# Query row loads of an attention visit: from SyncE's queue into ScalarE's instruction order

## The reference

```
for i in range(NL):                       # NL = 6, D = 128, H = 16 heads of HD = 8
    xn = _adaln(x, noise_emb, n1_w[i], n1_b[i])
    q, k, v = jnp.split(xn @ qkv_w[i].T, 3, axis=-1)
    q = _rope(q.reshape(B, L, H, HD)); k = _rope(k.reshape(B, L, H, HD))
    a = _attn(q, k, v.reshape(B, L, H, HD), src_mask).reshape(B, L, D) @ so_w[i].T   # softmax(q k / sqrt(HD)) v
    x = x + a
    ...   # the same against the 77 context rows (cross attention), then a GELU feed-forward
```

## Time and profile before

| what | value |
|---|---|
| three runs, median (lowest, highest) | 2218.05 us (2217.97, 2221.16) |
| profiled execution, its own time | 2213.04 us |
| its span, first to last instruction | 2211.2 us |
| PE busy | 1802.6 us (82%) |
| DVE busy | 1723.1 us (78%) |
| ACT busy | 1517.0 us (69%) |
| POOL busy | 1035.1 us (47%) |
| DMA traffic | 155.11 MB, mean 70 GB/s |

### The profile page before, as it was taken

How to read it: one execution, slowest core, us unless ns; L and a number is a source line. 1 busy time by engine, 2 the same in 40 slices (tenths; PEclk the granted TensorE clock), 3 DMA queues, 4 the chain that set the end, 5 groups by cost and what they waited for, 6 DMA issues and landing times.

```text
span 2211.2 us, 40093 instructions
## 1 busy us (share of the span) xinstructions
PE 1802.6 (82%) x13138; PEld 767.3 (35%) x13138; DVE 1723.1 (78%) x4125; ACT 1517.0 (69%) x2808; POOL 1035.1 (47%) x1506
## 2 busy tenths in 40 slices
PE   4564185278999999999999999999999999999662
PEld 2332174122333333333333333333333333333231
DVE  6766111588899888998888987889988889888777
ACT  2443031156888888888888887888888888889553
POOL 2443712824454555454554554554545545444532
PEclk9766598569999999999999999999999999999785
DMA  3001122322423343423533325333244232432100
GB/s 101 1 0 38 56 86 76 85 52 69 96 66 67 88 101 79 92 59 70 108 82 83 79 55 112 86 68 88 53 106 94 71 81 68 90 86 59 30 2 20
DMA packets 153736, 155.11 MB, mean 70 GB/s; under 512 B 32247, under 2 KB 137523, under 8 KB 153523
## 3 DMA queue, kind: packets, MB, share of 16 engines
q1 hardware_dynamic: 151487, 148.34, 28.8%
q0 software_dynamic: 2048, 4.20, 0.7%
HBM read 82.15 MB, written 67.85 MB: 68 GB/s over the span
## 4 chain that ended last, share of the span: by engine, by line
PE 55%; DVE 10%; DMA 9%; POOL 6%; ACT 5%; issue 3%; SPq 2%; POOLq 0%; DVEq 0%; ACTq 0%
PE ps L1357 14%; DMA q<-scratch_queries 8%; PE ps L1310 7%; PE ps L1321 6%; DVE smax L1878 4%; PE ps L1459 4%; PE ps L1469 4%; ACT big L1586 4%; PE ps L1368 3%; PE ps L1433 2%; PE ps L600 2%; PE ps L610 2%; PE ps L1393 2%; PE ps L1344 2%; PE ps L1332 1%
## 5 line engine op out<-in xcount | busy, mean ns | idle before, releaser
L1586 ACT ACTIVATE big<-ps 128x512 f32<-128x512 f32 x1920 | 1009.6, 613 | 214.9 <-PE ps L1321 204.6
L1878 DVE TENSOR_REDUCE smax<-ps 128x1 f32<-128x512 f32 x1536 | 966.7, 684 | 175.8 <-PE ps L1310 123.3
L1357 PE MATMUL ps<-big,vaug 128*32 128x512 f32 x3072 | 430.4, 634 | 2.3 <-ACT xnT L1594 1.2
L1310 PE MATMUL ps<-k,q 49*128 49x512 bf16 x1536 | 294.7, 394 | 80.9 <-DMA q<-scratch_queries 56.1
L1321 PE MATMUL ps<-q,k 52*128 52x512 bf16 x1536 | 291.1, 392 | 9.2 <-DVE smax L1878 3.3
L1310 PEld LDWEIGHTS ps<-k,q 49*128 49x128 bf16 x1536 | 76.1, 94 | 314.4 <-DVE smax L1878 153.1
L1789 POOL CAST mparts<-smax 128x16 bf16<-128x16 f32 x96 | 19.2, 200 | 324.4 <-DVE smax L1878 324.4
L1886 DVE TENSOR_REDUCE maxima<-ps 128x4 f32<-128x308 f32 x384 | 157.2, 469 | 9.4 <-PE ps L1344 5.9
L1321 PEld LDWEIGHTS ps<-q,k 52*128 52x128 bf16 x1536 | 78.9, 94 | 215.5 <-issue 65.4
L1775 POOL TENSOR_TENSOR rot<-rot,cs 128x512 f32<-128x512 f32 x72 | 92.0, 1277 | 103.3 <-DVE rot L1897 103.3
L1780 POOL TENSOR_TENSOR hat<-rot,rparts 128x512 f32<-128x512 f32 x72 | 82.6, 1161 | 70.6 <-ACT rparts L1634 70.6
(11 more groups left out here) (312 smaller groups left out, 2938.2 us busy)
## 6 DMA issues: line engine op xcount, KB each, us to landing
k<-scratch_keys SPq DMA_DIRECT2D x48, 384.0 KB
q<-scratch_queries SPq DMA_DIRECT2D x48, 384.0 KB, 8.1
cq<-scratch_cross_queries SPq DMA_DIRECT2D x48, 384.0 KB, 6.0
scratch_keys<-rparts SPq DMA_DIRECT2D x24, 384.0 KB, 2.5
scratch_queries<-rparts SPq DMA_DIRECT2D x24, 384.0 KB
scratch_cross_queries<-rparts SPq DMA_DIRECT2D x24, 384.0 KB
scratch_keys<-rparts SPq DMA_DIRECT2D x24, 256.0 KB, 2.2
scratch_queries<-rparts SPq DMA_DIRECT2D x24, 256.0 KB
```

Of the source, the lines that this page charges most:

```text
L1310: last = nc.tensor.matmul(out[u], m.q6[rows, v % 2, 2 * g + pr, qt * P:(qt + 1) * P], m.k6[rows, v % 2, 2 * g + pr, :], start=True, stop=True)
L1357: last = nc.tensor.matmul(m.ps[32 * j:32 * j + 32, pv_bank, :], of_head(m.vaug, v % 2 * TB + kt, g, j), of_quad("self", q)[:, j, :], start ...
L1586: nc.scalar.activation(of_quad(kind, p // 2)[:, p % 2 * 2 + u, :], bank("exp" if kind == "self" else "cross exp", p, u), ACT.Exp, scale=sc ...
L1878: nc.vector.tensor_reduce(m.smax[:, n % 2, qt, u, pr:pr + 1], bank("max", i, u), AX.X, ALU.max).then_inc(s_read["self"], 1)
```

## The change

The two query loads leave SP's program and become a piece of ACT's, "ACT load queries", with the same number in the plan as before (-32643 in the part "next"). In ACT's order this puts them behind exp 13 of visit v - 1 and ahead of scale cross of visit v - 2 (visits 4 to 23). Their waits go with them. The two DMAs of the mask rows stay on SP and move into load_keys, ahead of the two key loads. So SP's order becomes mask, mask, key, key where it was key, key, mask, mask, query, query. No arithmetic changes and no bytes.

```diff
-    "SP load queries": (-32643,),
+    "ACT load queries": (-32643,),
...
-            def load_queries(v):
+            def load_keys(v):
                 b, i = v % B, v % 2
+                sp.wait_ge(x_stored["key"], 48 * (v + 1))
                 if v >= 2:
                     sp.wait_ge(scores["self"], PER_VISIT * (v - 1))
                 for u in range(2):
                     lo = u * ROW_BLOCK
                     sp.dma_start(m.k6[lo + ROW_MASK:lo + ROW_SHIFT, i],
                                  a["neg_mask"][b:b + 1, :].unsqueeze(1).to_broadcast([1, PAIRS, S])).then_inc(k_loaded[i], 16)
-                sp.wait_ge(x_stored["query"], 48 * (v + 1))
-                src = a["queries"][b].rearrange("(i u r) c n -> u (r c) i n", u=2, r=HD)
-                for u in range(2):
-                    sp.dma_start(m.q6[u * ROW_BLOCK:u * ROW_BLOCK + ROW_MASK, i], src[u]).then_inc(q_loaded[i], 16)
-
-            def load_keys(v):
-                b, i = v % B, v % 2
-                sp.wait_ge(x_stored["key"], 48 * (v + 1))
-                if v >= 2:
-                    sp.wait_ge(scores["self"], PER_VISIT * (v - 1))
                 src = a["keys"][b].rearrange("(i u r) c n -> u (r c) i n", u=2, r=HD)
                 for u in range(2):
                     sp.dma_start(m.k6[u * ROW_BLOCK:u * ROW_BLOCK + ROW_MASK, i], src[u]).then_inc(k_loaded[i], 16)
...
-                for i in due("SP load queries", now):
-                    load_queries(i)
...
+            def load_queries(v):
+                b, i = v % B, v % 2
+                if v >= 2:
+                    act.wait_ge(scores["self"], PER_VISIT * (v - 1))
+                act.wait_ge(x_stored["query"], 48 * (v + 1))
+                src = a["queries"][b].rearrange("(i u r) c n -> u (r c) i n", u=2, r=HD)
+                for u in range(2):
+                    act.dma_start(m.q6[u * ROW_BLOCK:u * ROW_BLOCK + ROW_MASK, i], src[u]).then_inc(q_loaded[i], 16)
...
+                for v in due("ACT load queries", now):
+                    load_queries(v)
                 for v in due("ACT copy values", now):
                     copy_values(v)
```

## The result

The change makes the kernel slower: 2279.8 us (median of four runs, 2277.2 to 2281.1) against 2218.0 us before (2213.2 to 2221.2), a ratio of 1.0279 with the interval 1.0258 to 1.0300, or 62 us. The profiled execution took 2278.7 us with a span of 2277.0 us, 65.8 us more than the span before. The forecast was 2287 us in a range of 2250 to 2328.

The account below looks back on a forecast made before the run. PE (82% busy) was taken as the bound, waiting on query loads. Wait 57 + stores 8 + clock 8 - given back 4 = +69 us on 2213.0 profiled makes 2282, as a median 2287; range 2250 to 2328.

Parts of the forecast that it names:

- The place in ACT's order decides: ACT's first query load behind exp 13's wait for scores 13: issued at 802.44 in visit 6, before the running exponentials end.
- The rival in which a DMA waits for its engine: ACT issues the query loads only when its running exponentials are finished: +35 us more, 2322 us; chance 17%.
- The window of 1.8 us: From ACT's issue behind scores 13 to the end of scores 14, when loads could land for nothing, in each visit.
- The landing: Second query load on ACT lands 6.9 us behind its own issue, at 809.8 in visit 6 (bounds 808.9 and 810.6).
- +57 for the wait: PE ahead of the max scores, 20 visits: waits 5.5 us for the queries instead of 2.70, +57 us in all.
- "quick landing" rival: Second query load lands in 6.0 us or less, no more clock drop, no stores in the way: +24, 2242; chance 13%.
- The clock: TensorE behind PE's wait: half clock in all 20 visits instead of 15, 5 x 1.7 = +8 us.
- The rival in which the clock suffers twice: TensorE gets a second slow stretch in each visit: +34 us, 2321 us; chance 5%.
- The context stores: SP's stores in 5 of 20 visits, in flight beside the query loads, delay them: 5 x 1.5 = +8 us (0 to 15).
- The masks: Mask rows ahead of SP's key loads: keys start 1.40 us later but land 5 us before the queries; costs nothing.
- Given back: Other waits of PE made up while it rests for the queries: -4 us, of 14 us at most over 20 visits.

## Why the prediction was right

Direction, mechanism and size held: +69 us were forecast, and it is 62 between the medians and 65.8 in the span. By its steps:

**The place in ACT's order decides: right.** ACT's issue came 0.10 us behind the end of scores 13, as forecast, 1.7 us before the exponentials ahead of it were done (811.96 + 1.11). The rival in which a DMA waits for its engine (17%) is dead. That SP with the same wait loses as much (1.0241), and ACT with an early place and the masks in the wait almost nothing (1.0037), shows that lateness is the cause and the issuer is not.

**The window of 1.8 us: right.** From ACT's issue to the end of scores 14 it is 811.34 to 813.13, 1.79 us.

**The landing: the term that was most off, and too long.** 7.4 us from the first issue to the second landing were forecast (0.5 for the first issue, 6.9 for the second load). In visit 6 it is 6.8 (811.34 to 818.16), and the 20 waits average 5.0 instead of 5.5 us. The terms of +57 for the wait and +8 for the stores beside it measured 100.0 - 53.9 = +46 us together. The first issue takes 0.31 us there, not the 0.46 us of the earlier trace rows, and the second load lands 6.5 us behind its own issue (811.68 to 818.16), not 6.9. That is so although more is moved meanwhile: 207 to 240 GB/s in this visit, one of the five with context stores, where the pair from which it was estimated ran alone at 155. The "quick landing" rival (13%) was thus half right in its size (4.6 us of waiting, 5.5 in the forecast, 5.0 measured) and wrong in its sum, since it left the clock out.

**The clock: right in kind, too small.** A drop was expected in the five visits that had none, 8 us. PE's busy time grew by 21.6 us instead: the five got their drop, and in most of the others more work runs at 0.50 behind the longer wait (4.5 us instead of 3.4 in visit 6). In visits 4 to 23 together it is 94 us of work instead of 54, and half of the difference is 20 us. The two runs with filling matmuls give the same by another way (27 to 30 us lost before, 48 to 52 after). The rival in which the clock suffers twice was right in kind, with 6.8 us at 0.50 in 17 of the 20 visits, but its price (34 us more, 42 in all) was too high, since part of that time lies in the wait.

**The context stores: too large.** They were to delay the queries by 8 us in all. It is mostly the stores that are late: in visit 6 the one issued at 812.87 lands after 5.3 us, where it took 3.4 before. From the first issue to the second landing the queries take 7.1 us on average in the five visits with stores and 6.6 in the others: 2 us in all, which are part of the 46. The 155 GB/s at which the stores were reckoned was no limit: with them in flight 207 to 240 were moved.

**The masks: nothing, as forecast.** The run with the masks behind the keys shows no difference. But the same order costs 2.2% where the queries follow the keys at once. The forecast holds only because the queries are late, as its reason said (the keys 5 us ahead of them).

**Given back: about as said.** 46 + 22 = 68 us of terms against 65.8 us of span: 2 us, forecast 4.

So the sum came out better than its terms: wait and stores were 19 us too large (65 for 46), the clock 14 too small (8 for 22), and what is given back 2 too large; 69 - 19 + 14 + 2 = 66. That the mechanism came out was no luck, but that the sum is off the span's 66 us by only 3 is: two errors of 19 and 14 us went opposite ways.

## What to carry to other kernels

When a load moves to another engine's program, compare two times in the trace: when that program reaches its place (the last wait ahead of it, and who ends it) and when the consumer arrives; here the difference was 1.8 us for a transfer of 6.8. For loads that together keep the DMA engines full, it is the first issue that counts, and even 1.4 us of small DMAs ahead of it delay the last landing; neither the order among these loads nor the issuer mattered here. And where TensorE waits several microseconds in every round, look at the granted clock behind the wait: filling matmuls gave back 0.9% here without any load landing sooner.

## What the runs showed that was not expected

- Where keys and queries follow each other, the four loads of a visit take 11.5 to 11.8 us from the first issue to PE's start, on average over visits 4 to 23, in either order, on one queue or two, and with the masks just ahead or not (in visit 6: 795.18 to 806.84 before, 797.25 to 808.92 with the queries first, 805.37 to 817.11 with the queries early on ACT and the masks out of the way).
- The issue of a query load takes 0.33 us on ACT in the median and 0.46 us on SP before, but that isn't shown to be a matter of the engine: with the loads late on SP, the first of the pair takes 0.31 us in visit 6, as on ACT. The second of ACT's pair took 1.15 us in visit 6, and up to 1.26 us elsewhere; in the run with the late loads on SP an issue took up to 1.07. ACT's exponentials went on meanwhile.
- Three filling matmuls in each wait (56.8 us of work) made the kernel 20 us faster, and behind the wait of visit 6 the granted clock then was 1.00 where it had been 0.50.
- What stays open: what lowers the clock ahead of visit 4 where ACT issues the loads early, which costs 7 us there, and whether a number of filling matmuls fitted to each visit's wait would give more.
